# A gated cross-attention layer: key projections ahead of the remainders, bounds of Wq and of the ffn matrix on other engines, the second tile's x earlier

## The reference

```
q = layernorm(x) @ Wq ; k = ctx @ Wk ; v = ctx @ Wv        (split into 16 heads)
attn = softmax(q k^T / 8) ; a = (attn v) @ Wo + bo
x = x + tanh(g_xattn) * a
idx = argmax(log_softmax(logits) - log(-log(u)))           (one of 8 ffn matrices)
x = x + tanh(g_ffn) * (layernorm(x) @ W[idx] + b[idx])
```

## Time and profile before

| | |
|---|---|
| median of 3 runs | 1044.67 us (1043.48, 1044.67, 1044.71) |
| profiled execution | 1044.16 us, its span 1042.4 us |
| TensorE busy | 1027.5 us, 99% of the span |
| VectorE, ScalarE, POOL busy | 847.8, 749.1, 443.0 us (81%, 72%, 42%) |
| granted TensorE clock | 1.00 |
| chain that ended last, by engine | TensorE 89%, VectorE 4%, ScalarE 3%, DMA 2% |

### The profile page before, as it was taken

The page is one execution under the profiler, slowest core; times in us unless marked ns, Lnnn a source line. Parts: engine busy times, 40 slices in busy tenths (PEclk is TensorE's granted clock), DMA queues, the critical chain, the costliest instruction groups (busy, mean ns, idle before and its releaser), DMA issues.

```text
span 1042.4 us, 21853 instructions
## 1 busy us (share of the span) xinstructions
PE 1027.5 (99%) x6074; PEld 587.0 (56%) x6074; DVE 847.8 (81%) x1800; ACT 749.1 (72%) x2720; POOL 443.0 (42%) x637
## 2 busy tenths in 40 slices
PE   9998999999999999999999999999999999999998
PEld 7634455555555555555555555555555555555555
DVE  4677988888888888888888887888888887888876
ACT  3778877777677677776777677766776677767761
POOL 1686344444443344444433344444433344444422
PEclk9999999999999999999999999999999999999999
DMA  8414566665566665665566666655566656655656
GB/s 323 101 21 111 107 127 125 143 126 125 111 134 137 139 135 125 141 123 114 117 137 136 136 134 129 142 119 111 128 137 136 136 126 138 136 116 111 133 110 142
DMA packets 383073, 135.02 MB, mean 130 GB/s; under 512 B 361930, under 2 KB 362750, under 8 KB 382974
## 3 DMA queue, kind: packets, MB, share of 16 engines
q1 hardware_dynamic: 382974, 134.09, 59.8%
HBM read 27.48 MB, written 16.78 MB: 42 GB/s over the span
## 4 chain that ended last, share of the span: by engine, by line
PE 89%; DVE 4%; ACT 3%; DMA 2%; SPq 1%; issue 1%; POOL 0%; DVEq 0%; ACTq 0%
PE banks L1405 82%; PE banks L1638 3%; ACT work L902 1%; PE banks L1515 1%; DMA fold_area<-in_L_xattn_Wo 1%; PE banks L1451 1%; PE banks L1523 1%; PE banks L1504 1%; DVE work L449 1%; ACT vw_area L850 0%; DMA work<-work 0%; DVE vw_area L1110 0%; DVE fold_area L1121 0%; DVE red L1030 0%; DVE work L1209 0%
## 5 line engine op out<-in xcount | busy, mean ns | idle before, releaser
L902 ACT ACTIVATE work<-banks,red,cst 128x77 f32<-128x77 f32 x1024 | 410.3, 430 | 83.3 <-DVE red L1200 83.2
L1405 PE MATMUL banks<-fold_area,work 128*128 128x456 f16 (+1 forms) x2304 | 405.4, 335 | 2.8 <-DMA work<-work 2.0
L1405 PE MATMUL banks<-vw_area,work 128*128 128x512 f16 x1674 | 371.4, 379 | 0.9 <-DMA work<-work 0.9
L1405 PEld LDWEIGHTS banks<-fold_area,work 128*128 128x128 f16 x2304 | 225.2, 98 | 171.4 <-DMA work<-work 2.9
L1405 PEld LDWEIGHTS banks<-vw_area,work 128*128 128x128 f16 x1674 | 163.6, 98 | 186.0 <-DMA work<-work 1.8
L449 DVE SCALAR_TENSOR_TENSOR work<-work 128x256 f16<-128x256 f32 (+3 forms) x443 | 240.8, 578 | 1.3 <-ACT work L798 0.6
L902 ACT ACTIVATION_READ_ACCUMULATOR work<-banks,red,cst 128x1 f32 x1024 | 224.5, 219 | 0.0
L1198 DVE TENSOR_REDUCE stats<-banks 128x6 f32<-128x462 f32 (+1 forms) x192 | 112.1, 584 | 102.3 <-PE banks L1405 102.2
L1405 PE MATMUL banks<-work 128*128 128x256 f16 x1302 | 162.4, 272 | 0.7 <-DVE work L1285 0.5
L1405 PEld LDWEIGHTS banks<-work 128*128 128x128 f16 x1302 | 126.8, 98 | 31.8 <-DVE work L1285 0.7
L733 POOL TENSOR_TENSOR stats<-stats,cst 128x1 f32<-128x1 f32 x64 | 12.6, 196 | 281.5 <-DVE stats L1234 281.5
(11 more groups left out here) (150 smaller groups left out, 818.0 us busy)
## 6 DMA issues: line engine op xcount, KB each, us to landing
work<-in_x SPq DMA_DIRECT2D x64, 256.0 KB, 2.8
out<-work SPq DMA_DIRECT2D x63, 256.0 KB, 2.2
work<-work SPq DMA_TRANSPOSE x253, 3.1
fold_area<-in_L_xattn_Wo SPq DMA_DIRECT2D x4, 512.0 KB, 9.1
work<-in_L_ffn_W SPq DMA_DIRECT2D x2, 1024.0 KB, 8.4
fold_area<-in_L_xattn_Wq SPq DMA_DIRECT2D x2, 1024.0 KB, 14.5
fold_area<-in_L_xattn_Wv SPq DMA_DIRECT2D x3, 512.0 KB, 6.5
fold_area<-in_L_xattn_Wk SPq DMA_DIRECT2D x2, 768.0 KB, 12.3
```

What stands on the lines that cost most here:

```text
L902: nc.scalar.activation(probs_of(place, place + 1), s_heads(m, k)[:, h - h0, :], ACT.Exp, bias=nmx[:, h:h + 1], scale=exp_scale, accum_out= ...
L1405: mm = nc.tensor.matmul(ps, lhs(l), rhs(r), start=first and n == 0, stop=last and n == 2, skip_group_check=onto)
```

## The change

The list of visits has all four `PROJECT` first, then `REMAINDER` 0, the spread of KK and WQ, `TURN` 0 and `VALUE` 0, and the first two key folds before `REMAINDER` 2. The spread of WF becomes a visit of its own (`SPREAD` 1) in the place of `PASS` 0. From `KEY` 2 on all visits keep their places. ScalarE's bounds are two passes over Wq and two over the ffn matrix, instead of four over Wq; VectorE reduces the other half of Wq, instead of the ffn matrix. The spread of VV comes after `PROJECT` 1. x of tile 1 is loaded at the start (the transposed values, vT, move up by one slot of x to make room; the turned x of tile 1 gets a room that is free after the staged values), its moments are taken at `KEY` 4, its scale at `KEY` 7, its normalization at `KEY` 15 and its high part at `KEY` 17; its low part stays in step 0. The scale of tile 0 moves behind `REMAINDER` 2. On SP the wait for all value folds moves behind the turns of x, and the turn of tile 1's x no longer waits for the staged keys.

```
-        vT = at(D, HP * BJ).rearrange(...)
+        vT = at(2 * D, HP * BJ).rearrange(...)
-        xT_second = xr[:, RING - 1, :].bitcast(F16)...
+        xT_second = at(free, D).bitcast(F16)...
-        PARTS = [5, 4, 4, 4, 1]
+        PARTS = [5, 4, 4, 3, 2]
-        VISITS = [(PROJECT, 0), (PROJECT, 1), (PROJECT, 2), (REMAINDER, 0), (VALUE, 0), (PROJECT, 3), (REMAINDER, 1), (VALUE, 1),
-                  (SPREAD, 0), (TURN, 0), (REMAINDER, 2), (VALUE, 2), (REMAINDER, 3), (KEY, 0), (KEY, 1), (VALUE, 3), (TURN, 1),
-                  (PASS, 0), (KEY, 2), (KEY, 3), (VALUE, 4), (PASS, 1), ...
+        VISITS = [(PROJECT, 0), (PROJECT, 1), (PROJECT, 2), (PROJECT, 3), (REMAINDER, 0), (SPREAD, 0), (TURN, 0), (VALUE, 0),
+                  (REMAINDER, 1), (KEY, 0), (KEY, 1), (VALUE, 1), (REMAINDER, 2), (TURN, 1), (VALUE, 2), (REMAINDER, 3), (VALUE, 3),
+                  (SPREAD, 1), (KEY, 2), (KEY, 3), (VALUE, 4), (PASS, 1), ...
...
 SP
-            sp.dma_start(xr[:, 0, :], x[0, 0:P, :]).then_inc(x_loaded[0], 16)
+            for n in range(2):
+                sp.dma_start(xr[:, n, :], x[n, 0:P, :]).then_inc(x_loaded[n], 16)
...
-            sp.wait_ge(v_folded, 4 * VALUES)
-            sp.dma_start(xr[:, 1, :], x[1, 0:P, :]).then_inc(x_loaded[1], 16)
             sp.wait_ge(bo_set, 16 * 2 * B)
             turn_x(0, 0)
             sp.wait_ge(v_stage_lo, len(STAGED_VALUES))
             sp.wait_ge(side_lo, 4 * KT)
             sp.dma_start(wf_raw, ...).then_inc(wf_again, 16)
-            sp.wait_ge(k_stage_lo, key_staged_before(UNITS))
             turn_x(0, 1)
+            sp.wait_ge(v_folded, 4 * VALUES)
...
 POOL
-                if (kind, n) == (REMAINDER, 1):
+                if (kind, n) == (REMAINDER, 2):
                     x_scale(0, 0)
-                if (kind, n) == (KEY, 24):
+                if (kind, n) == (KEY, 7):
                     x_scale(0, 1)
...
 ScalarE
+            def query_bounds():
+                act.wait_ge(floor_set, 1)
+                act.wait_ge(wq_loaded[0], 16)
+                act.wait_ge(v_done, HP)
+                for k in range(KT // 2):
+                    nc.scalar.activation(wv_raw[:, k, :], wq_raw[:, k, :], ACT.Abs, accum_out=part_of(WQ, 1 + k)).then_inc(parts_ready[WQ], 1)
+            def ffn_bounds():
+                act.wait_ge(wf_loaded, 16)
+                for n, junk in enumerate(...):
+                    rows = wf_raw[:, n * KT // 2:(n + 1) * KT // 2, :].rearrange("p k n -> p (k n)")
+                    nc.scalar.activation(junk, rows, ACT.Abs, accum_out=part_of(WF, n)).then_inc(parts_ready[WF], 1)
             copy_k(0)
+            copy_k(1)
             act.wait_ge(scale_v_ready, 1)
...
-                if (kind, n) == (PROJECT, 2):
-                    query_bounds(0)
-                if (kind, n) == (VALUE, 0):
-                    query_bounds(1)
+                if (kind, n) == (PROJECT, 2):
+                    query_bounds()
+                if (kind, n) == (PROJECT, 3):
+                    ffn_bounds()
...
+                if (kind, n) == (KEY, 15):
+                    x_normalized(0, 1)
+                if (kind, n) == (KEY, 17):
+                    x_high(0, 1)
...
 VectorE
             largest(VV)
+            key_part(0)
             power_of_two(VV, 3)
...
-            dve.wait_ge(wf_loaded, 16)
-            part(WF, 0, wf_raw)
-            largest(WF)
-            key_part(0)
             key_part(1)
...
+                if (kind, n) == (PROJECT, 2):
+                    dve.wait_ge(wq_loaded[1], 16)
+                    part(WQ, 0, wq_raw[:, KT // 2:KT, :])
+                    largest(WQ)
                 if (kind, n) == (PROJECT, 3):
                     largest(KK)
-                    largest(WQ)
...
-                    power_of_two(WF, first, P)
+                if (kind, n) == (SPREAD, 1):
+                    power_of_two(WF, pair_of(SPREAD, 1))
-                if (kind, n) == (PROJECT, 3):
+                if (kind, n) == (KEY, 1):
+                    largest(WF)
                     x_moments(0, 0)
...
-                if (kind, n) == (KEY, 1):
+                if (kind, n) == (VALUE, 3):
                     x_low(0, 0)
-                if (kind, n) == (KEY, 24):
+                if (kind, n) == (KEY, 4):
                     x_moments(0, 1)
-                if (kind, n) == (KEY, 25):
                     dve.wait_ge(x_stats, 2)
                     x_variance()
...
 TensorE
-                if (kind, n) == (PROJECT, 0):
+                if (kind, n) == (PROJECT, 1):
                     spread(VV, 3)
-                if kind == SPREAD:
-                    spread(WF, pair_of(SPREAD), P)
+                if (kind, n) == (SPREAD, 1):
+                    spread(WF, pair_of(SPREAD, 1))
+                if (kind, n) == (SPREAD, 0):
                     spread(KK, pair_of(SPREAD))
                     spread(WQ, pair_of(SPREAD) + 1)
```

More of the change, by code:

```diff
@@ L122, in flamingo_layer @@
         xr = at(0, RING * D).rearrange("p (r n) -> p r n", r=RING)
-        vT = at(D, HP * BJ).rearrange("p (h n) -> p h n", h=HP)
+        vT = at(2 * D, HP * BJ).rearrange("p (h n) -> p h n", h=HP)
         c = Carve(work)
@@ L165, in flamingo_layer @@
         k_stage = [c.take(2 * BS).rearrange("p (e n) -> p e n", e=2),
-                   at(D + HP * BJ, 2 * BS).rearrange("p (e n) -> p e n", e=2)]
-        assert c.at <= x2T_at and D + HP * BJ + 2 * BS <= RING * D
+                   at(2 * D + HP * BJ, 2 * BS).rearrange("p (e n) -> p e n", e=2)]
+        assert c.at <= x2T_at and 2 * D + HP * BJ + 2 * BS <= RING * D
         free = x2T_at + KT * D
+        xT_second = at(free, D).bitcast(F16).rearrange("p (s k n) -> p s k n", s=2, k=KT)
         v_stage = [at(start, 2 * D).rearrange("p (e n) -> p e n", e=2) for start in (x2T_at, free)]
@@ L179, in flamingo_layer @@
         VV, WO, KK, WQ, WF = range(5)
-        FROM = [0, 6, 11, 16, 21]
-        PARTS = [5, 4, 4, 4, 1]
+        FROM = [0, 6, 11, 16, 20]
+        PARTS = [5, 4, 4, 3, 2]
         amax, top, pow2, rcp = red[:, 24:29], red[:, 29:34], red[:, 34:39], red[:, 39:44]
@@ L364, in flamingo_layer @@
         PROJECT, REMAINDER, VALUE, SPREAD, TURN, KEY, PASS = range(7)
[L365 to L367 removed]
+        VISITS = [(PROJECT, 0), (PROJECT, 1), (PROJECT, 2), (PROJECT, 3), (REMAINDER, 0), (SPREAD, 0), (TURN, 0), (VALUE, 0),
+                  (REMAINDER, 1), (KEY, 0), (KEY, 1), (VALUE, 1), (REMAINDER, 2), (TURN, 1), (VALUE, 2), (REMAINDER, 3), (VALUE, 3),
+                  (SPREAD, 1), (KEY, 2), (KEY, 3), (VALUE, 4), (PASS, 1), (KEY, 4), (KEY, 5), (VALUE, 5), (TURN, 2), (KEY, 6), (KEY, 7), (VALUE, 6),
                   (KEY, 8), (KEY, 9), (VALUE, 7), (TURN, 3), (KEY, 10), (KEY, 11), (VALUE, 8), (KEY, 12), (KEY, 13), (VALUE, 9),
@@ L808, in copy_k @@
                                banks[:, pair_of(PROJECT, n):pair_of(PROJECT, n) + 2, 0:BS]).then_inc(k_copied, 1)
-            def query_bounds(half):
+            def query_bounds():
                 act.wait_ge(floor_set, 1)
-                act.wait_ge(wq_loaded[half], 16)
+                act.wait_ge(wq_loaded[0], 16)
                 act.wait_ge(v_done, HP)
-                for k in (2 * half, 2 * half + 1):
-                    nc.scalar.activation(wv_raw[:, k, :] if k < CT else fold_area[:, A_WORDS + CT * ID:A_WORDS + CT * ID + ID], wq_raw[:, k, :],
-                                         ACT.Abs, accum_out=part_of(WQ, k)).then_inc(parts_ready[WQ], 1)
+                for k in range(KT // 2):
+                    nc.scalar.activation(wv_raw[:, k, :], wq_raw[:, k, :], ACT.Abs, accum_out=part_of(WQ, 1 + k)).then_inc(parts_ready[WQ], 1)
+            def ffn_bounds():
+                act.wait_ge(wf_loaded, 16)
+                for n, junk in enumerate((wv_raw[:, CT - 1, :], fold_area[:, A_WORDS + CT * ID:A_WORDS + CT * ID + ID])):
+                    rows = wf_raw[:, n * KT // 2:(n + 1) * KT // 2, :].rearrange("p k n -> p (k n)")
+                    nc.scalar.activation(junk, rows, ACT.Abs, accum_out=part_of(WF, n)).then_inc(parts_ready[WF], 1)
             copy_k(0)
+            copy_k(1)
             act.wait_ge(scale_v_ready, 1)
@@ L827, in side_copied @@
                 if t == 0:
-                    act.wait_ge(parts_ready[WF], 1)
+                    act.wait_ge(parts_ready[WF], PARTS[WF])
                 if t >= 2:
@@ L872, in _ @@
             for kind, n in VISITS:
-                if kind == PROJECT and n > 0:
+                if kind == PROJECT and n > 1:
                     copy_k(n)
+                if (kind, n) == (PROJECT, 2):
+                    query_bounds()
+                if (kind, n) == (PROJECT, 3):
+                    ffn_bounds()
                 if kind == REMAINDER:
@@ L976, in step @@
                     lone_high(NT - 1)
-                if valid(o1):
+                if valid(o1) and not is_tile(o, m, 0):
                     x_normalized(o1, m1)
@@ L1486, in taken_before @@
                 elif kind == SPREAD:
```

(2 more changed lines are left out.)

1 line of the change is left out of this document (removed).

## The result

The changed kernel takes 1047.82 us (median of 8 runs, 1046.77 to 1048.51) against 1044.44 us for the kernel before (8 runs): 3.38 us or 0.31% slower, ratio 1.0031 with a 95% interval of 1.0022 to 1.0040. Its profiled execution took 1047.60 us, span 1045.8.

A forecast was written before the change was run, and what follows sets the result against it. TensorE is full from 118 us, so only the second attention's start, set by the first exponential, counts. Delay 2.3 + 0.2 - 0.5 led to an exponential 1.65 us late: 1046.3 us, range 1045.3 to 1047.2, eight in ten 1043.5 to 1048.2.

The forecast's parts named there:

- rival (b): POOL stays late, delaying the ffn reload; VectorE's last key split slows the step before exponentials, 0.7; 1047.3 to 1048.4; chance 0.20.
- slower: Outcome beyond the 0.2% (2.1 us) that measurement can tell, above 1046.8 us; chance 0.32.
- step 3: Near 50 us: ScalarE waits 2.1 us for POOL's tile 0 scale, TensorE waits twice, V4 2.3 late (1.6 to 2.8).
- the high part: In the folds: tile 1's high part on ScalarE pushes V12's copy; 0.2 us taken, bounds 0 and 1.0.
- Step 1: All projections first: the 0.79 us wait is gained, P3 ends at 32.24 and R0 at 34.16.
- Step 2: Spread of KK, near 34 to 35 us: TensorE newly waits 1.1 us for VectorE's Wq reduction and last key part.
- Step 4: Folds to 88 us: the 2.3 delay is handed on, plus 0.2, less 0.5 at the end; scores at 89.9.
- Step 5: Scores to first exponential: score maxima and reloaded ffn matrix both ready at 93.0 to 93.2, against 91.50; +1.65 us.
- Step 6: The 1.28 us wait for tile 1's turned x before 95.50 goes, but is waited again; worth nothing at 118 us.
- Rival (a): The stall is soaked up before 50 us, V4 near 50.1, exponentials 0.9 early; 1043.8 us; chance 0.15.

The follow-up runs named there:

- e10: Changed kernel with the first tile's x_scale back behind side split 1 and the three two-tensor scale operations rewritten with one SBUF tensor; 1044.05 us.
- e6: Changed kernel with three repairs: first tile's x_scale back behind side split 1, scale operations with one SBUF tensor, TURN 0 ahead of the spread of KK; 1043.45 us.
- e4: Changed kernel with TURN 0 ahead of the spread of KK and WQ, its copy right behind scale_q; 1046.86 us, 6 of 11 runs at a clock below 1.
- e1: Changed kernel with the first tile's x_scale on POOL put back behind side split 1; 1045.57 us.
- e5: Changed kernel with three scale operations written with one SBUF tensor and a per-partition scalar instead of two SBUF tensors; 1046.60 us.
- e3: Kernel before the change with VectorE's six scale operations moved from KEY 12 to KEY 13; 1045.98 us.
- e7: Kernel before with one-SBUF-tensor scale operations and the change's early handling of tile 1's x; visit order, bounds and tile 0 as before; 1044.66 us.
- e2: Changed kernel with VectorE's six scale operations moved from KEY 12 to KEY 17; 1050.16 us (5 runs), clock below 1.
- e8: Kernel before the change with only the scale operations rewritten to one SBUF tensor; 1044.92 us.
- e9: e6 with value unit 13 instead of 14 as the last that POOL splits, meant to issue the ffn matrix reload earlier; 1043.13 us.

## Why the prediction was right, and what it missed

1047.82 lay within the eight-in-ten range of 1043.5 to 1048.2 but outside the forecast's own range, which ended at 1047.2. It lay at the price of rival (b), which had 0.20, and "slower" had only 0.32. The direction and the stall of step 3 were right for the reason given. That the time was met as closely as it was is in part luck: a loss of 1.29 us was missing from the sum, and V4's delay was put 0.68 too high and the high part 0.2. By the steps, in the profiles and counted from the spread of WO, so without the later start:

- **Step 1** held: TensorE came from the spread of WO to R0 in 12.60 us; I had 13.06 (19.18 to 32.24).
- **Step 2** held: wait of 1.04 us (1.1 said). Its worth is 0.60 us between e10 and e6; e4's 0.96 is blurred by the clock.
- **Step 3** held in kind and place: ScalarE waited 2.50 us for POOL (2.1 said), then TensorE 1.42 and 0.64. V4 came 2.86 late, 1.62 without the start (2.3 said, 1.6 to 2.8 allowed). The size was taken too high, by 0.68; 0.46 of that is what step 1 gained more. Undoing it gave 2.25 us (e1).
- **Step 4** is the one that failed: "I leave the 2.3", and 0.2 for the high part. The high part cost nothing, and the end gained 0.44 (0.5 said). But between K14 and V10 another 1.29 us were lost (69.92 to 73.00, before 67.07 to 68.86). I had followed POOL's lateness only as far as the reload, and had not asked which VectorE operations now lay beside POOL's splits. In the kernel before the scale operations stood in a gap of POOL's, from 67.17 to 68.06 (VectorE's first with two tensors, POOL's rows around it, and TensorE's V10):

```profile
67.69 0.15 DVE L1135 SCALAR_TENSOR_TENSOR cst<-red 128x1 f32<-128x1 f32 x1
```

```profile
65.32 1.85 POOL L692 TENSOR_TENSOR fold_area<-work,fold_area 128x608 f16<-128x608 f32 x1
68.06 1.04 POOL L680 CAST vw_area<-work 128x1024 f16<-128x1024 f32 x1 [0.89 <-ACT work L848]
```

```profile
68.86 1.09 PE L1515 MATMUL banks<-fold_area,work 64*64 64x512 f32 x8 [0.31 <-DVE fold_area L1121]
```

In the changed kernel POOL had no gap there. e5 and e3 show it from both sides, 1.2 and 1.5 us. The stall of step 3 is not needed for it (e1). The second tile's x_scale, 1.2 us of POOL's work put behind K7, is enough to take most of the gap in the old order: e7 has it at 61.19 to 62.45, and of the 0.89 us of POOL's wait there 0.20 are left, up to 68.53. I had counted this x_scale for the reload alone.
- **Step 5**: from the start of the scores to the first exponential 3.45 us (3.25 said, 3.61 before). The matrix landed at 93.53, 5.28 us after its issue (my 5.33 for before was misread: ScalarE's wait of 0.15 us ended at 89.39 with the landing, which makes 5.48), and ScalarE was done with it at 94.86; VectorE's maxima came 0.18 later. Both conditions met, as said, 1.9 us later than said.
- **Step 6** was wrong and cost nothing: the wait before the second scores stayed, 1.13 us. The low part of tile 1, 92.30 to 94.02, took 1.72 us beside POOL's last key split, so the turn was issued at 94.13. In the profiles of e1, e5 and e7 it landed in time, and the same wait appeared before the first attention (1.31, 1.31 and 1.30 us), the second attention still 26.5 us after the exponential.
- **The start.** 1.24 us of the 3.54 between the two profiles lie before the spread of WO. No term stood for it. In eight profiles of the new order it was at 19.21 to 20.73, in four of the old one at 19.18 to 19.89; whether the change shifts it, these few don't show. They do show that the new order hands most of it on: from there to the spread of KK it took 15.62 or 15.63 us in the four profiles of the changed kernel, e1, e5 and e10, with starts from 19.47 to 20.42, and 15.86 in e2, which started earliest, at 19.21. The old order has a cushion in the 0.79 us wait before the spread of VV: against before, that spread came 0.06 us later in e8 for a start 0.69 later, 0.38 in e3 for 0.71, and 0.46 in e7 for 0.69. The exponential of e8 was 0.22 later, 0.14 of it from the new form at V10. So the 2.30 us below are taken against a profile that started early; against e8 the distance of the changed kernel is 2.77 us longer. The six runs of it at a clock of 1.00 are 3.1 us above the kernel before.

In sum, from the spread of WO: 1.62 + 1.29 - 0.44 - 0.16 = 2.31, read directly 74.62 - 72.32 = 2.30. The forecast of 1.65 lacked the 1.29 and had 2.3 where 1.62 was measured, and 0.2 for the high part, which cost nothing.

Rival (a) fell with e1's trace and e7. Rival (b) had the price right, 1047.3 to 1048.4, and POOL's lateness, but a wrong way for it: of its second place, VectorE being held up, I put 0.7 on the small step before the exponentials (it took 0.23 us) and nothing on the scale operations. The Trainium skill's section "VectorE Performance Modes" (Advanced Engine Details and Errata), on which the prediction drew, speaks of two-port modes, and under the conditions that it lists an operation on one column would not be expected to suffer. The Trainium skill's GPSIMD Engine Reference, section "Specifications", adds VectorE instructions with two SBUF inputs; e5 and e3 agree with that, 0.2 us for the form with one tensor and up to 2.09 for the form with two.

## What to carry to other kernels

When an edit makes an engine late, look beyond the buffers that it hands over: list what the other engine does in the gaps that vanish, and for products of single columns prefer the form with one SBUF tensor where GpSimd may be busy. It is no cure at any width: a TENSOR_SCALAR with one SBUF tensor, but on six columns, took 0.23 us at 94.78, with POOL idle, and 1.24 us at 104.88, to within 0.04 us of the end of a POOL instruction (VectorE and POOL of the changed kernel; the kernel before has 1.25):

```profile
104.88 1.24 DVE L1211 TENSOR_SCALAR red<-stats,cst 128x6 f32<-128x6 f32 x1
```

```profile
104.80 1.28 POOL L717 TENSOR_TENSOR work<-work 128x512 f32<-128x512 f32 x1
```

A short operation put behind a 3.35 us one in an ordered queue delays also what its consumer's queue holds behind it. Read a gap from the kernel that will run, not from the one whose waits the edit removes (e2). Before a run's time is put down to its edit, look at the clock in its stages (e2, e4).

## What was not expected of the hardware

**One-column operations held up for the length of a POOL instruction.** A product of two SBUF columns took 0.13 to 0.15 us where it began between two POOL instructions, even in a gap of 0.08 us, and 0.54, 0.58, 0.59, 0.73, 0.93, 0.98, 2.08 and 2.09 us where it began during one, in e1 to e4 and the changed kernel up to the end of that instruction, within 0.05 us.

**The clock after waits of 1.0 to 2.0 us.** The granted clock of a whole run was below 1.00 in none of the 81 runs of the kernel before that accompanied the experiments and in none of 11 each of e6, e7, e8 and e9, but in 2 of 8 of the changed kernel, 3 of 11 of e1 and of e5, 2 of 11 of e3, 1 of 11 of e10, 6 of 11 of e4 and 5 of 5 of e2. The kernel before has a wait of 1.07 us in its folds; in the others, the longest wait in the folds was 1.54 to 1.99 us in the changed kernel, e1 to e4, and in e5 and e10, whose waits there are shorter (up to 1.42 and 0.85), there is the 1.04 us wait at the spread of KK. In e2 the clock is 0.64 from 36 to 40 us, behind that wait. e4 shows one case, its columns those of the earlier trace rows:

```profile
72.50:75.50 3.00, 3.00 (x12) 0.76 (x12) 0.60 (x1) 0.92 (x1) 2.92 (x3) 0.50 0.02 5
```

```profile
72.45 1.98 PE L1527 MATMUL banks<-fold_area,work 64*64 64x512 f32 x8 [1.58 <-DVE fold_area L1132]
74.37 1.38 PE L1535 MATMUL banks<-work 64*128 64x304 f32 x4
75.68 1.09 PE L1527 MATMUL banks<-fold_area,work 64*64 64x512 f32 x8
```

After the wait of 1.58 us the granted clock is 0.50 for three microseconds, the lower of the two levels, 1.2 GHz, and V10 takes 1.98 us instead of 1.09. From V10 to V11 it took 3.23 us, in the changed kernel 1.73: 1.5 us for this one fall. From V11 on the durations are the usual ones again. In e5 the three such runs took 1047.44 to 1047.94 us, the eight others 1045.86 to 1047.06: a wait in TensorE's way costs its length, and in some runs 1 to 2 us more. In the 3.38 us this part is small: the two runs of the changed kernel at 0.998 took 1048.51 and 1048.39 us, the six others 1046.77 to 1048.22 with a median of 1047.57. Why the clock falls in one run and not in the next, no run here shows.
